# Deformable-sampling column weights on all 128 partitions at once, and sampling products at two row positions

## What is computed

```python
ys = hh + dy + off[..., 0]            # per pixel, group and tap
xs = ww + dx + off[..., 1]
y0, x0 = (jnp.floor(ys), jnp.floor(xs))
for oy in (0.0, 1.0):
    for ox in (0.0, 1.0):
        yy, xx = (y0 + oy, x0 + ox)
        wgt = (1.0 - jnp.abs(ys - yy)) * (1.0 - jnp.abs(xs - xx))
        ...
        out = out + jnp.where(valid, wgt, 0.0)[..., None] * g     # g: the value at (yy, xx)
return jnp.einsum('npkgc,npkg->npgc', out, mk)
```

## Time and profile before

| | |
|---|---|
| median of 2 runs | 1320.55 us (1318.87 to 1322.22) |
| span of the profiled execution (no other time of it is given) | 1326.9 us, mean granted TensorE clock 0.888 |
| busy: PE, DVE, ACT, POOL | 1078.8 (81%), 836.9 (63%), 583.9 (44%), 394.8 us (30%) |
| one pass of the loop, first tap unit to the next pass's | 150.7 us |

### The profile page before, as it was taken

The page is one execution under the profiler, slowest core; times in us unless marked ns, Lnnn a source line. Parts: engine busy times, 40 slices in busy tenths (PEclk is TensorE's granted clock), DMA queues, the critical chain, the costliest instruction groups (busy, mean ns, idle before and its releaser), DMA issues.

```text
span 1326.9 us, 17127 instructions
## 1 busy us (share of the span) xinstructions
PE 1078.8 (81%) x5184; PEld 728.2 (55%) x5184; DVE 836.9 (63%) x1592; ACT 583.9 (44%) x1245; POOL 394.8 (30%) x340
## 2 busy tenths in 40 slices
PE   2574799689977899689987799679987799779857
PEld 2341575456645676456755576446755576556534
DVE  2786467955597456955588465975588456864232
ACT  1422543463435544454435634464435634454233
POOL 0274014610275004620157003640166003640000
PEclk9955699879997899869997999899997999789958
DMA  4122000000000000000000000000000000000000
GB/s 133 49 69 61 19 1 1 1 2 3 0 0 0 5 0 0 0 2 3 0 0 0 4 0 0 0 2 3 0 0 0 5 0 0 0 0 3 0 1 2
DMA packets 5326, 12.32 MB, mean 9 GB/s; under 512 B 1118, under 2 KB 2342, under 8 KB 5094
## 3 DMA queue, kind: packets, MB, share of 16 engines
q1 hardware_dynamic: 4782, 9.02, 2.6%
q10 hardware_dynamic: 494, 2.81, 0.7%
HBM read 11.30 MB, written 0.52 MB: 9 GB/s over the span
## 4 chain that ended last, share of the span: by engine, by line
PE 58%; DVE 17%; issue 11%; ACT 6%; POOL 6%; DMA 1%; DVEq 0%; POOLq 0%; SPq 0%; ACTq 0%
PE ps_y L546 18%; PE ps_h L521 6%; POOL sb_acc L1068 5%; PE ps_h L535 4%; PE ps_h L522 4%; PE ps_h L536 4%; PE ps_t L451 4%; DVE sb_prod L902 4%; PE ps_m L437 4%; PE ps_t L452 3%; PE ps_t L419 2%; PE ps_h L501 2%; DVE sb_hx L886 2%; ACT sb_xg L736 2%; PE ps_t L501 1%
## 5 line engine op out<-in xcount | busy, mean ns | idle before, releaser
L1068 POOL TENSOR_TENSOR sb_acc<-sb_acc,sb_prod 128x512 f32<-128x512 f32 x256 | 332.4, 1320 | 235.0 <-DVE sb_prod L902 234.1
L750 ACT ACTIVATE sb_hid<-ps_h 114x512 f32<-114x512 f32 (+1 forms) x256 | 150.2, 595 | 287.0 <-PE ps_h L522 286.6
L973 DVE TENSOR_TENSOR sb_hid<-ps_h,sb_hid 114x512 f32<-114x512 f32 (+1 forms) x256 | 172.1, 685 | 154.7 <-ACT sb_hid L750 150.6
L451 PE MATMUL ps_t<-sb_bdh,sb_hx 128*128 128x512 f32 x288 | 157.8, 548 | 70.2 <-DVE sb_prod L902 66.6
L546 PE MATMUL ps_y<-sb_hid,sb_w2s 114*64 114x256 f32 x768 | 205.8, 392 | 0.0
L902 DVE TENSOR_TENSOR sb_prod<-ps_t,sb_hy 128x512 f32<-128x512 f32 x256 | 170.7, 683 | 32.1 <-POOL sb_acc L1068 20.5
L451 PEld LDWEIGHTS ps_t<-sb_bdh,sb_hx 128*128 128x128 f32 x288 | 63.7, 221 | 136.5 <-DVE sb_prod L902 108.2
L736 ACT ACTIVATE sb_xg<-sb_xn,sb_gt 128x128 f32<-128x128 f32 x384 | 120.1, 390 | 25.0 <-DVE sb_gt L961 25.0
L452 PE MATMUL ps_t<-sb_bdl,sb_hx 128*128 128x512 f32 x288 | 129.9, 451 | 0.0
L546 PEld LDWEIGHTS ps_y<-sb_hid,sb_w2s 114*64 114x64 f32 x768 | 90.3, 136 | 64.7 <-issue 10.7
L521 PE MATMUL ps_h<-sb_xh,sb_w1s 128*114 128x256 f32 x384 | 117.3, 327 | 0.7
(11 more groups left out here) (169 smaller groups left out, 1756.6 us busy)
## 6 DMA issues: line engine op xcount, KB each, us to landing
sb_hid<-in_w1T SPq DMA_DIRECT2D x16, 171.0 KB, 3.1
sb_hid<-in_w3T SPq DMA_DIRECT2D x16, 171.0 KB, 3.0
sb_w2s<-in_w2T ACTq DMA_DIRECT2D x1, 1368.0 KB
sb_hid<-in_u1T SPq DMA_DIRECT2D x4, 256.0 KB, 3.9
sb_hid<-in_u2T SPq DMA_DIRECT2D x4, 256.0 KB, 3.7
sb_omx<-in_omxT ACTq DMA_DIRECT2D x1, 612.0 KB
sb_xT<-in_x SPq DMA_DIRECT2D x8, 64.0 KB, 2.1
sb_u3s<-in_u3T ACTq DMA_DIRECT2D x1, 512.0 KB
```

The costliest lines, as they stand in the source:

```text
L451: mm(tb[u % 2][:, :], w, bdh[:, h, :], start=True, stop=False)
L750: af(hid[0:ch, j % RING, :], h1[j % 2][0:ch, :], ACT.Silu).then_inc(s_act_s, 1)
L973: v.tensor_tensor(hid[0:ch, j % RING, :], h3[j % 2][0:ch, :], hid[0:ch, j % RING, :], ALU.mult).then_inc(s_dve_hid, 1)
L1068: g.tensor_tensor(acc[:, t, h, :], acc[:, t, h, :], prod[:, u % 2, :], ALU.add).then_inc(s_pool_acc, 1)
```

## The change

The omx weights are laid out so that one product per tap gives the distances of all 8 groups on 128 partitions (8 groups x 16 columns), without the doubling. ACT works in place in mb, on 256 columns. DVE makes the high part (hxh) and the low part (hxl) as tensors of their own, from mb. Columns k on PE wait for column weights k-1, since mb now holds them. The high and low parts lie no longer in different rows, so a sampling product of a half has 64 rows and there are four terms (high and low of both factors) for each half. The even unit issues all eight products for both halves, one half at rows 0 to 63 into tb[0] and the other at rows 64 to 127 into tb[1], in turns; it waits for all of DVE's products before it. The odd unit issues nothing on PE. DVE's and POOL's work in the tap steps stays as it is.

```diff
-        omx = sb("omx", [AUG, K * NH * P])
+        omx = sb("omx", [AUG, K * P])
-        bdh = sb("bdh", [P, NH, GH * GC * H], f32r)
-        bdl = sb("bdl", [P, NH, GH * GC * H], f32r)
+        bdh = sb("bdh", [P, GH * GC * H], f32r)
+        bdl = sb("bdl", [P, GH * GC * H], f32r)
-        hat = sb("hat", [P, NH * PIX])
-        hx = sb("hx", [P, 3, NH, PIX], f32r)
+        hxh = sb("hxh", [P, 3, PIX], f32r)
+        hxl = sb("hxl", [P, 3, PIX], f32r)
...
-                    pe.wait_ge(s_act_abs, count(K * n + k))
-                for h in range(NH):
-                    o = (k * NH + h) * P
-                    last = mm(mb[:, h * PIX:(h + 1) * PIX], omx[:, o:o + P], dwT[:, :], start=True, stop=True)
-                last.then_inc(s_pe_xr, 1)
+                    pe.wait_ge(s_dve_hx, count(K * n + k))
+                mm(mb[:, 0:PIX], omx[:, k * P:(k + 1) * P], dwT[:, :], start=True, stop=True).then_inc(s_pe_xr, 1)
...
-                if u >= 2:
-                    pe.wait_ge(s_dve_p, count(UNITS * n + u - 1))
-                w = hx[:, k % 3, h, t * P:(t + 1) * P]
-                mm(tb[u % 2][:, :], w, bdh[:, h, :], start=True, stop=False)
-                mm(tb[u % 2][:, :], w, bdl[:, h, :], start=False, stop=True).then_inc(s_pe_t, 1)
+                if h == 0:
+                    if u >= 2:
+                        pe.wait_ge(s_dve_p, count(UNITS * n + u))
+                    terms = ((hxh, bdh), (hxh, bdl), (hxl, bdh), (hxl, bdl))
+                    for i, (w, bd) in enumerate(terms):
+                        for g in range(NH):
+                            rows = slice(g * GH * W, (g + 1) * GH * W)
+                            last = mm(tb[g][:, :], w[rows, k % 3, t * P:(t + 1) * P], bd[rows, :],
+                                      start=(i == 0), stop=(i == 3))
+                            if i == 3:
+                                last.then_inc(s_pe_t, 1)
...
             def columns(n, k):
                 act.wait_ge(s_pe_xr, count(K * n + k + 1))
-                if k > 0 or not isinstance(n, int):
-                    act.wait_ge(s_dve_hx, count(K * n + k))
-                af(hat[:, :], mb[:, :], ACT.Abs).then_inc(s_act_abs, 1)
+                af(mb[:, 0:PIX], mb[:, 0:PIX], ACT.Abs).then_inc(s_act_abs, 1)
                 act.wait_ge(s_act_abs, count(K * n + k + 1))
-                af(hat[:, :], hat[:, :], ACT.Relu, scale=-1.0, bias=1.0).then_inc(s_act_hat, 1)
+                af(mb[:, 0:PIX], mb[:, 0:PIX], ACT.Relu, scale=-1.0, bias=1.0).then_inc(s_act_hat, 1)
...
-                o = V(hx[:, k % 3, :, :], [[1, NH * PIX]])
-                v.tensor_copy(o, hat[:, :]).then_inc(s_dve_hr, 1)
+                v.tensor_copy(hxh[:, k % 3, :], mb[:, 0:PIX]).then_inc(s_dve_hr, 1)
                 dve.wait_ge(s_dve_hr, count(K * n + k + 1))
-                v.scalar_tensor_tensor(out=o, in0=o, scalar=negb[:, 0:1], in1=hat[:, :], op0=ALU.mult,
-                                       op1=ALU.add).then_inc(s_dve_hx, 1)
+                v.tensor_tensor(hxl[:, k % 3, :], mb[:, 0:PIX], hxh[:, k % 3, :], ALU.subtract).then_inc(s_dve_hx, 1)
```

More of the change, by code:

```diff
@@ L672, in diagonal @@
                 act.wait_ge(s_dve_bd, count(4 * n + 4))
-                af(bdh[:, :, :], acc[:, 0, :, :], ACT.Copy).then_inc(s_act_bh, 1)
+                af(bdh[:, :], acc[:, 0, 0, :], ACT.Copy).then_inc(s_act_bh, 1)
             def offsets(n):
@@ L868, in diagonal @@
                     for h in range(NH):
-                        o = V(acc[:, 0, h, b * (H // 2):GH * GC * H], [[1, H // 2], [GC * H, GH], [H, GC]])
-                        src = V(tb[b][:, h * GH * GC:2 * PIX], [[C, H // 2], [GC, GH], [1, GC]])
-                        v.tensor_tensor(o, src, V(gmask[:, :], [[0, H // 2], [1, GH], [0, GC]]), ALU.mult).then_inc(s_dve_bd, 1)
+                        rows = slice(h * GH * W, (h + 1) * GH * W)
+                        o = V(acc[rows, 0, 0, b * (H // 2):GH * GC * H], [[1, H // 2], [GC * H, GH], [H, GC]])
+                        src = V(tb[b][rows, h * GH * GC:2 * PIX], [[C, H // 2], [GC, GH], [1, GC]])
+                        v.tensor_tensor(o, src, V(gmask[rows, :], [[0, H // 2], [1, GH], [0, GC]]), ALU.mult).then_inc(s_dve_bd, 1)
                 dve.wait_ge(s_dve_bd, count(4 * n + 4))
                 dve.wait_ge(s_act_bh, count(n + 1))
-                v.tensor_tensor(bdl[:, :, :], acc[:, 0, :, :], bdh[:, :, :], ALU.subtract).then_inc(s_dve_bl, 1)
+                v.tensor_tensor(bdl[:, :], acc[:, 0, 0, :], bdh[:, :], ALU.subtract).then_inc(s_dve_bl, 1)
             def row_distances(n, t):
@@ L1101, in lay_out @@
     ky = np.repeat(np.arange(K) // 3 - 1, G)
-    big = ox.reshape(NH, GH, K, C + 1).transpose(3, 2, 0, 1)[:, :, :, None, :, None]
-    omx = T(np.broadcast_to(big, (C + 1, K, NH, 2, GH, W)).reshape(C + 1, K * NH * P))
-    kx = np.broadcast_to((np.arange(K) % 3 - 1)[:, None, None, None, None] - np.arange(W), (K, NH, 2, GH, W)).reshape(-1)
+    big = ox.transpose(2, 1, 0)[:, :, :, None]
+    omx = T(np.broadcast_to(big, (C + 1, K, G, W)).reshape(C + 1, K * P))
+    kx = np.broadcast_to((np.arange(K) % 3 - 1)[:, None, None] - np.arange(W), (K, G, W)).reshape(-1)
     L["omxT"] = np.concatenate([omx, np.stack([np.ones(kx.size), np.zeros(kx.size), kx]).astype(f)])
```

## The result

The changed kernel takes **1451.5 us** in the median of its two runs (1443.15 and 1459.80) against 1320.55: the ratio is 1.0985, interval 1.091 to 1.106. I had forecast +31 us; it is +131. The profiled execution is the one of 1459.80 us (span 1457.9, granted clock 0.852, before 0.888). Its span is 131.0 us longer than that of before, so what follows splits 131 us.

A forecast was written before the change was run, and what follows sets the result against it. DVE was taken to bound the tap stretch and PE's matmuls the rest; +4.0 us a pass gave +28 over seven, with +5 for the first image and -2 at the start +31, so 1352 us, range 1298 to 1458.

The forecast's parts named there:

- The lost alternation: Tap stretch: PE and DVE take turns at 17 borders, 1.25 us each, 21.3 us, or 15.6 after cover.
- the signs I named for it: Profile after: DVE's waits for PE grow from 6.9 to some 18 us, POOL's adds leave them, PE's waits grow.
- the sum: One loop pass: shorter column weights, gaps, old waits, new waits, switching, clock and column products together give +4.0 us.
- the walk: Both orders stepped through the tap stretch with the assumed durations: waits of 0.3 to 1 us elsewhere turn -2.0 into +3.3.
- switching and clock: Tap stretch: array shape changes (0.2 to 0.3 us a round trip) and PE's slower clock after waits, 1.6 us together.
- The gaps: DVE idle between pairs in the stretch: 21.3 us less 5.7 covered by other work; 6.0 of old waits go.
- the whole second half at half clock: Bad end for a pass: nine pairs at 2.14 us in place of 1.25, +10 us.
- The rest: Matmul-bound part of a pass outside the taps: two of nine column products there save 0.9 us.
- First image: Its taps, 66.8 us before: between -7 at full clock and +8 at half clock, taken as +5 us.
- B: Rival: the two row positions don't overlap, so each pair takes eight slots; 1450 us, chance 0.25.
- C: Rival: faster, as DVE's freed time removes new waits and a gap is 0.9 us; 1275 us, chance 0.13.
- the first case: Main forecast: positions overlap, turns cost a little more than shorter weights give; 1352 us, own range 1305 to 1390, chance 0.62.

The follow-up runs named there:

- turns_alone: Kernel before, only with units issued in pairs: the even unit issues both halves' 128-row products, the odd none; first bank released after two products; 1405.2 us.
- turns_late: As turns_alone, but both banks are released to DVE only after the fourth product; 1479.1 us.
- columns_alone: Changed kernel with the sampling products as before (two of 128 rows a unit, alternating banks), some terms left out; 1300.2 us.
- units_apart: Changed kernel, but each unit issues its own four 64-row products into its own bank, keeping the alternation; 1355.7 us.
- columns_later: columns_alone with column products k+2 one unit later in PE's order; 1277.5 us.
- three_terms: Changed kernel without the product of the two low parts, so three slots a pair for four; 1444.2 us.
- psum_later: psum_source with column products k+2 one unit later in PE's order; 1295.2 us, 0.980 of the kernel before.
- own_hat: Changed kernel, but ACT writes its results to SBUF again and column products wait for ACT's first pass only; 1446.7 us.
- psum_source: Kernel before, with ACT in place on 512 columns and column weights read from PSUM, old doubling and units kept; 1376.4 us.

## Why the prediction was wrong

**The sum of the causes.** The turns cost 83 us (turns_alone), the common release of both banks 74 (turns_late less turns_alone), the column part gives 22 (columns_alone): +135, and the change has +131. That they add up so well is partly luck, since the parts share waits and a clock; but each was run as one edit, and keeping the alternation (units_apart) takes back 96 of the 131.

**Right.** The two positions overlap, with a pair in 1.20 us. Copy and subtraction take 415 and 424 ns, beside POOL too (predicted: 0.79 us for the pair, start to start). DVE's work in the stretch fell by 10.7 us for 11.6. The lost alternation is the mechanism of the loss, and the signs I named for it are there: DVE's waits for PE grown, POOL's adds gone from its waits, PE waiting in return. The constants come 1.35 us earlier (DVE's row starts at 17.88 us) for 2. The mechanism was right, then, and the sizes were not.

**The step that failed** is "the sum", +4.0 us per pass: its terms for DVE's idle time were too small. Measured are 103.7 / 7 = +14.8 in the stretch (114.0 less the first image's 10.3) and 2.4 in the rest, 17.2. Its terms, in the pass of the windows above, as changes of DVE's idle time in the stretch (+26.0 measured; +16.5 forecast, which is 15.6 - 6.0 for gaps and old waits, 5.3 for waits found by the walk, 1.6 for switching and clock):

- *The gaps.* I had 15.6 us after 5.7 of cover, less 6.0 of old waits. Measured are 31.6 - 3.9 = 27.7 us of waits for 6.0, so +21.7 for +9.6. One gap at full clock is 1.37 us where I had 1.25; 17 borders have 1.6 in the mean, cover and half clock together. The 12.1 us too much are 17 x 0.12 = 2.0 of longer gaps, 7 of half clock (next item), and some 3 of cover, which by this sum was worth 2.6 us and not 5.7.
- *The clock.* I gave it a part of 1.6 us and put "the whole second half at half clock" at the end of my range. Eight of 18 pairs are at half clock; at 2.25 for 1.37 us these are, by my estimate, 8 x 0.88 = 7 us of the 21.7 in a pass, and PE's other work there slows too. The term should have followed from the turns: turns_alone, which has nothing else of the change, shows a clock of 0.76 to 0.78 in the stretches of the loop for the 0.85 to 0.92 of before. The size of this share is read from rows; no run isolates it.
- *The rest.* -0.9 forecast, +2.4 measured. Rests at a clock of 0.91 are 86 us long, the one at 460.0 to 542.1 us at 1.00 is 82.1 (before had 79.8 at 1.00).
- *First image.* +5 forecast, +10.3 measured (75.3 for 65.0 us).

**A cost I had not split off.** I priced the pair as one thing, with both banks late. In turns_alone the first bank is free for DVE after two products, and just that is worth 74 us. It is nearly half of the 158 us of turns_late, and it comes from filling the banks side by side, which is what the change is about.

**A gain I booked in full.** The 11.6 us of shorter column weights counted as if DVE alone set the stretch. columns_alone gives 2.1 us there, columns_later 5.5 (438.9 for 477.5 in seven): with DVE shorter, PE's waits and the wait at columns 4 set the end. I had seen that wait and priced it at 1 us with what follows; where units alternate it is worth 22 to 81 us a run. Set against the single runs, the forecast had some 130 us for the turns (16.5 in each of seven passes and 17 in the first image) and some 100 back from the column part (12.5 a pass, 12 in the first image, 2 at the start); the runs have 158 and 22. So by this account most of the 100 us that I missed lie in the gain, not in the turns. The two accounts cut the same loss in two ways and can't be added: where DVE's shorter work only makes it wait longer for PE, the windows book that as idle time.

**The rivals.** B stood at 1450 and 0.25; its time was met by another mechanism, which only its rows can tell. C fell with the gap: it needed a mean under 1.0 us, and 27.7 us over 17 borders are 1.6. The range held the time because B's price was in it, not because the first case reached so far.

**Open.** How much of the 131 us the clock takes was not run by itself: no run keeps PE at full clock through the turns. Why three_terms gives so little, and why the cover between pairs was worth so little, is argued only.

## What to carry to other kernels

Packing products of two banks side by side ties the release of both banks together and takes the alternation with the engine that reads them; each of the two cost more here than the shorter work gave, so release each bank when its own products are done, and issue unit by unit, since products at different rows found each other here anyway. Even so the layout lost 34 us (13 with the columns later); the gain came from reading PSUM with the old products (psum_later). When an engine's work in a stretch is shortened, ask what is late next before booking the gain, and price every new wait of PE with the half clock that can follow it. When a buffer is used in place, look at what is queued behind the new wait: one move in the order was worth 81 us.

## What the runs showed of the hardware that I had not expected

**Row positions are queues of their own.** In the changed kernel at columns 4, in order of time (L567 are the queries' products at rows 0 to 63, which stand ahead of tap (2,2), L452, in the program):

```profile
562.04 0.70 PE L567 MATMUL ps_h<-sb_flat,sb_xn2T 64*128 64x256 f32 x2
562.37 0.50 PE L452 MATMUL ps_t<-sb_bdh,sb_hxh 64*128 64x512 f32 x1
562.58 0.38 PE L567 MATMUL ps_h<-sb_flat,sb_xn2T 64*128 64x256 f32 x1
562.71 0.39 PE L452 MATMUL ps_t<-sb_bdl,sb_hxh 64*128 64x512 f32 x1
562.79 0.39 PE L567 MATMUL ps_h<-sb_flat,sb_xn2T 64*128 64x256 f32 x1
562.82 0.79 PE L452 MATMUL ps_t<-sb_bdh,sb_hxh 64*128 64x512 f32 x1
```

Tap (2,2) starts at 562.37, before two records of the queries at 562.58 and 562.79. Rows don't show a product's position, but the taps' other half starts its first product at 562.82, behind the queries, so it is the half at rows 64 to 127 that has run ahead of another step. The Trainium skill, "TensorE: Matmul & The Clock Gate", Part 3 (Packing small matmuls), has row groups overlap, and by the rows of the pairs the trace agrees, at two products per slot of 0.23 us. The same section has products start and end strictly in program order, and here the trace disagrees: 562.37 stands before 562.58.

**The source decides how a subtraction on DVE fares beside POOL.** It has the same 128x256 elements in own_hat and in the change (L889 above); one input, hxh, lies in SBUF in both, the other in SBUF in own_hat and in PSUM in the change. In own_hat, with the shortest, the median and the longest in ns:

```profile
L892 DVE TENSOR_TENSOR sb_hxl<-sb_hat,sb_hxh x72: 424/1388/1479, 49.2 to 1272.2; 128x256 fp32r<-128x256 f32 x72
```

The 41 of them that run beside one of POOL's adds take 1.38 to 1.48 us, the 31 with POOL idle 0.42 to 0.43. From PSUM all 72 take 424 to 426 ns, 46 of them beside an add. The 128x512 instruction has 1320 ns in the mean from SBUF (before) and 747 from PSUM (psum_source). For the copy it isn't so simple (own_hat and the change again): with 128x256 elements it takes 284 ns in the median from SBUF (280 to 1352) and 415 from PSUM (405 to 425).

**The column of the granted clock isn't always right.** In the first image's window it shows 1.00, where it was 0.61 before; the products there last as long as at half clock (0.63 us at 72.90). I read the clock from the lengths of products where it mattered.
